# Conditioning on 32x32 parts of the array, GpSimd casting the shared first weights, and a new deal of banks and of VectorE's first work

## The reference, cut to what matters

```python
w = weights[conditions]                       # 32 batches, each a 32x32 matrix
xc = einsum('bct,bcd->bdt', x, w)             # x is (32, 32, 256): 1024 tokens of 256
logits = xc @ gate_w; top 2 of 8 experts; capacity 160 tokens of an expert and choice
h = gelu(buf @ w1[e] + b1[e]); y = h @ w2[e] + b2[e] + gelu(buf @ wd[e]) @ wu[e]
sh = gelu(xc @ sw1 + sb1) @ sw2 + sb2 + gelu(xc @ swd) @ swu
out = x + sum over the 2 choices of weight * y + 0.2 * sh
```

## Time and profile before

| | us |
|---|---|
| three runs | 180.92, 179.42, 179.10 (median 179.42) |
| the profiled execution | 179.35 |
| its span (first to last instruction) | 177.6 |
| TensorE busy | 172.2 |
| VectorE, ScalarE, GpSimd busy | 149.7, 145.7, 96.4 |

### The profile page before, as it was taken

How to read it: one execution, slowest core, us unless ns; L and a number is a source line. 1 busy time by engine, 2 the same in 40 slices (tenths; PEclk the granted TensorE clock), 3 DMA queues, 4 the chain that set the end, 5 groups by cost and what they waited for, 6 DMA issues and landing times.

```text
span 177.6 us, 4056 instructions
## 1 busy us (share of the span) xinstructions
PE 172.2 (97%) x1410; PEld 167.5 (94%) x1410; DVE 149.7 (84%) x332; ACT 145.7 (82%) x323; POOL 96.4 (54%) x110
## 2 busy tenths in 40 slices
PE   5899999999999999999999999999999999999994
PEld 5797789999999999999999999999999999999993
DVE  5578999999996989879889699898999999989822
ACT  3369889805878997998899799999899999998920
POOL 5900448310447663087977948868947555264700
PEclk9999999999999999999999999999999999999999
DMA  4595000749938493595788859579688778686232
GB/s 129 128 351 174 0 0 2 242 145 315 326 76 304 111 303 84 238 251 68 258 289 120 284 161 182 134 278 229 142 292 191 196 258 151 238 259 75 29 65 94
DMA packets 25885, 31.84 MB, mean 179 GB/s; under 512 B 4572, under 2 KB 22392, under 8 KB 25864
## 3 DMA queue, kind: packets, MB, share of 16 engines
q1 hardware_dynamic: 21720, 26.22, 46.0%
q0 software_dynamic: 3904, 5.25, 16.7%
q10 hardware_dynamic: 240, 0.10, 0.2%
HBM read 26.31 MB, written 5.24 MB: 178 GB/s over the span
## 4 chain that ended last, share of the span: by engine, by line
PE 91%; DVE 4%; DMA 3%; issue 1%; DVEq 0%
PE y_ps L1040 14%; PE y_ps L1039 14%; PE y_ps L1038 14%; PE hid_ps L1038 9%; PE hid_ps L1039 9%; PE hid_ps L1040 9%; PE turn_ps L1038 4%; PE turn_ps L1040 4%; PE turn_ps L1039 4%; PE turn_ps L1207 2%; DMA cond_g<-in_L_cond_weights,itok_col 2%; PE hid_ps L1066 1%; DMA itok_col<-in_itok_B 1%; PE turn_ps L1066 1%; PE row_ps L1223 1%
## 5 line engine op out<-in xcount | busy, mean ns | idle before, releaser
L733 DVE TENSOR_TENSOR hid_l<-gelu_f,hid_h 128x320 fp32r<-128x320 f32 (+2 forms) x88 | 43.6, 510 | 10.9 <-ACT hid_h L628 10.2
L477 POOL DMA_INDIRECT out_rows<-y_row,slot_tok x23 | 38.1, 1655 | 24.7 <-DVE y_row L919 10.1
L463 POOL DMA_INDIRECT slot_in<-slot_rows,slot_src x23 | 31.0, 1348 | 18.4 <-DVE slot_src L889 7.9
L1038 PE MATMUL y_ps<-w_h,hid_h 128*128 128x256 f32 (+2 forms) x128 | 36.2, 283 | 0.0
L1039 PE MATMUL y_ps<-w_l,hid_h 128*128 128x256 f32 (+2 forms) x128 | 36.1, 282 | 0.0
L1040 PE MATMUL y_ps<-w_h,hid_l 128*128 128x256 f32 (+2 forms) x128 | 36.1, 282 | 0.0
L1038 PE MATMUL hid_ps<-xs_h,w_h 128*128 128x248 f32 (+6 forms) x96 | 27.6, 287 | 0.0
L627 ACT ACTIVATE gelu_f<-hid_ps,bias_s 128x320 f32<-128x320 f32 x48 | 26.2, 546 | 1.3 <-PE hid_ps L1040 1.1
L1039 PE MATMUL hid_ps<-xs_l,w_h 128*128 128x248 f32 (+6 forms) x96 | 27.2, 283 | 0.0
L1040 PE MATMUL hid_ps<-xs_h,w_l 128*128 128x248 f32 (+6 forms) x96 | 27.2, 283 | 0.0
L710 DVE TENSOR_TENSOR w_l<-w_raw,w_h 128x512 fp32r<-128x512 f32 x40 | 27.1, 712 | 0.0
(11 more groups left out here) (240 smaller groups left out, 445.6 us busy)
## 6 DMA issues: line engine op xcount, KB each, us to landing
w_raw<-in_L_ffn_w SPq DMA_DIRECT2D x16, 1024.0 KB, 5.2
w_raw<-in_L_ffn_sw SPq DMA_DIRECT2D x3, 1024.0 KB, 5.3
x_in<-in_x SPq DMA_DIRECT2D x2, 512.0 KB, 3.8
w_raw<-in_L_ffn_sw SPq DMA_DIRECT2D x2, 512.0 KB, 6.0
slot_rows<-token_row SPq DMA_DIRECT2D x2, 512.0 KB, 4.1
wu_raw<-in_L_ffn_wu SPq DMA_DIRECT2D x24, 32.0 KB
out_rows<-base SPq DMA_DIRECT2D x1, 512.0 KB, 4.8
slot_in<-slot_rows,slot_src POOLq DMA_INDIRECT x23
```

The lines of the kernel that those rows point to most:

```text
L463: pool.indirect_dma_start(out=slot_in[par][0:n, s, :], out_offset=None, in_=x_rows, in_offset=bass.IndirectOffsetOnAxis(ap=slot_src[0:n, e ...
L477: pool.indirect_dma_start(out=out, out_offset=bass.IndirectOffsetOnAxis(ap=slot_tok[0:n, e, s:s + 1].bitcast(U32), axis=0), in_=y_row[0:n, ...
L733: dve.tensor_tensor(hid_l[:, j - 1, 0:n], gelu_f[:, j % 3, 0:n], hid_h[:, j - 1, 0:n].bitcast(F32), ALU.subtract).then_inc(hid_split, 1)
L1038: pe.matmul(out_ap, l_h, r_h, start=start, stop=False)
```

## The change

Seven things are done at once.

1. `cond_diag` goes. The blocks lie in `cond_b` (32 columns for each tile), and 32 float32 matmuls of a 32x32 stationary block by 32x256 of `x_in`, 16 for each half, write token *rows*: block `g` of a tile reads partitions 32g to 32g+31 and writes partitions 32t to 32t+31 of bank `g` of its half (`tokens_ps`).
2. ScalarE and VectorE each copy two of a half's four banks to `token_row`, 16 transposes (1077) turn these into the old `xct` layout, in `xct_ps`, and the casts and remainders are read from there with a reordered pattern. `make_rows`, `keep_xct` and the late `copy_rows` go.
3. The rows go to HBM in eight transfers right after they are copied, not in two after the hidden tiles.
4. GpSimd casts all four chunks of the shared first weights; ScalarE casts none, and makes the two copies of the scores.
5. `hid_banks` is dealt anew for the shared tiles, `COUNT_AT` becomes 5 and `MAP_AT` 4, the ring of gelu buffers has five entries (the two new ones in `cond_g`), and the first output tile waits for an earlier gelu.
6. VectorE does its four `w1_chunk` in a row, and the first split between the two choices; one more split stands ahead of `side_data`.
7. SyncE waits for the first half of `x_in`, not for `cond_g`, before it issues the second half. Gelus, input casts and remainders of the sixth and later ranks of experts are cut to the most tokens such a rank can have (`MOST`; 292 and 256 columns in place of 320 for the last two).

```diff
-COUNT_AT = 4
-MAP_AT = 2
+COUNT_AT = 5
+MAP_AT = 4
+RING = 5
+MOST = [min(SLOTS, K * T // (r + 1)) for r in range(E)]
@@
+        tokens_ps = [[hid_ps[2], y_ps[0], row_ps, turn_ps[1]], [hid_ps[0], turn_ps[0], hid_ps[1], y_ps[1]]]
+        xct_ps = [[hid_ps[2], row_ps], [hid_ps[0], hid_ps[1]]]
@@
             if u == 0:
-                six = [hid_ps[2], y_ps[1], y_ps[0], hid_ps[0], hid_ps[1], turn_ps[1]]
-                return six + six[:HT - len(six)]
+                return y_ps + [hid_ps[2], hid_ps[0], hid_ps[1], row_ps, hid_ps[2], hid_ps[0], hid_ps[1]]
             if u == 1:
-                return [row_ps] + [hid_ps[j % 3] for j in range(1, HT)]
+                return [turn_ps[1]] + [hid_ps[j % 3] for j in range(1, HT)]
@@
-            sp.wait_ge(cond_in, 16)
+            sp.wait_ge(x_loaded[0], 16)
             sp.dma_start(x_in[:, HTILES:NT, :], x_v[:, HTILES:NT, :]).then_inc(x_loaded[1], 16)
@@
+            for c in range(CHUNKS):
+                pool.wait_ge(w1_in if c < CHUNKS // 2 else w1b_in, 16)
+                pool.tensor_copy(w1_h[0][:, :, c * FC:(c + 1) * FC],
+                                 w1_raw[:, :, c * FC:(c + 1) * FC]).then_inc(w1_hi, 1)
@@
-                if u == 0 and j < 3:
-                    pass
-                else:
-                    act.wait_ge(hid_split, hid_count(u, j) - 3)
+                if hid_count(u, j) > RING:
+                    act.wait_ge(hid_split, hid_count(u, j) - RING)
@@
-                for k in range(KD):
-                    dst = hid_ps[k] if h == 0 else turn_ps[k]
-                    for t in range(HTILES):
-                        ins = pe.matmul(dst[:, t * P:(t + 1) * P], x_in[:, h * HTILES + t, k * P:(k + 1) * P],
-                                        cond_diag[:, h * HTILES + t, :], start=True, stop=True)
-                    ins.then_inc(xct_made, 1)
...
+                for t in range(HTILES):
+                    for g in range(SPT):
+                        block = slice(g * C, (g + 1) * C)
+                        ins = pe.matmul(tokens_ps[h][g][t * C:(t + 1) * C, 0:D],
+                                        cond_b[block, h * HTILES + t, :], x_in[block, h * HTILES + t, :],
+                                        start=True, stop=True)
+                ins.then_inc(tokens_made, 1)
+            for h in range(2):
+                for i, g in enumerate(ROWS_TURNED):
+                    pe.wait_ge(rows_by_act, h * len(ROWS_ON_ACT) + i // 2 + 1)
+                    pe.wait_ge(rows_by_dve, h * len(ROWS_ON_DVE) + i // 2 + 1)
                     for k in range(KD):
...
+                        ins = pe.transpose(xct_ps[h][k][:, g * P:(g + 1) * P],
+                                           token_row[:, h * SPT + g, k * P:(k + 1) * P], ident[:, :])
```

More of the change, by code:

```diff
@@ L58 @@
 ON_ACT, ON_POOL = (3, 2), (1, 0)
+ROWS_ON_ACT, ROWS_ON_DVE = (0, 1), (2, 3)
+ROWS_TURNED = (0, 2, 1, 3)
 OUT_OF_REACH = -1.0e30
@@ L374, in _ @@
             for h in range(2):
[L375 to L377 removed]
+                sp.wait_ge(rows_by_act, (h + 1) * len(ROWS_ON_ACT))
+                sp.wait_ge(rows_by_dve, (h + 1) * len(ROWS_ON_DVE))
+                for t in range(HTILES):
+                    sp.dma_start(x_rows_v[h * HTILES + t], token_row[t * C:(t + 1) * C, h * SPT:(h + 1) * SPT, :]).then_inc(
+                        x_rows_out[h], 16)
             load_first(1)
@@ L645, in _ @@
                         "p (k e) -> p k e", k=K), ACT.Copy).then_inc(used_copied, 1)
-            for b in range(NT // 2):
-                copy_rows(b)
             act.wait_ge(centred, 1)
@@ L738, in _ @@
             dve.wait_ge(cond_spread, 1)
+            for g in range(SPT):
+                dve.tensor_copy(*spread_part(g)).then_inc(blocks_dve, 1)
             for h in range(2):
-                for g in range(SPT):
-                    dve.tensor_copy(*spread_part(h, g)).then_inc(diag_dve, 1)
+                dve.wait_ge(tokens_made, h + 1)
+                for g in ROWS_ON_DVE:
+                    dve.tensor_copy(*row_part(h, g)).then_inc(rows_by_dve, 1)
             dve.wait_ge(gate_in, 16)
@@ L943, in _ @@
             wu_part(0, 0)
-            for j in range(6, HT):
-                split_tile(0, j, HALF)
-                if j < HT - 1:
-                    w2_chunk(j - 6, 0, 0)
+            w2_chunk(0, 0, 0)
+            split_tile(0, 6, HALF)
+            w2_chunk(1, 0, 0)
+            split_tile(0, 7, HALF)
             w2_chunk(2, 0, 0)
             w2_chunk(3, 0, 0)
+            split_tile(0, 8, HALF)
             place_tokens()
@@ L1044, in _ @@
             with pe.Fori(0, WARM_UP) as _:
-                for _ in range(10):
-                    pe.matmul(y_ps[0][:, 0:P], ones[:, :], ones[:, :], start=True, stop=True)
+                for i in range(10):
+                    pe.matmul(y_ps[0][:, i % 4 * P:(i % 4 + 1) * P], ones[:, :], ones[:, :], start=True, stop=True)
             pe.wait_ge(ident_made, 2)
@@ L1102, in count_before, with shared_low @@
                 ins.then_inc(pos_made, 1)
+            def shared_low(h, x_h, x_l, cols, n):
+                pe.wait_ge(gate_lo, 1)
+                dst = hid_bank(h, 0)[0:LOW_GATE, 0:n]
+                for k in range(KD):
+                    pe.wait_ge(xct_hi, h * KD + k + 1)
+                    pe.matmul(dst, low_gate_h[:, k, :], x_h[:, k, cols], start=(k == 0), stop=False)
+                    pe.matmul(dst, low_gate_l[:, k, :], x_h[:, k, cols], start=False, stop=False)
+                for k in range(KD):
+                    pe.wait_ge(xct_lo, h * KD + k + 1)
+                    ins = pe.matmul(dst, low_gate_h[:, k, :], x_l[:, k, cols], start=False, stop=(k == KD - 1))
+                ins.then_inc(hid_made, 1)
             def hidden(u, j, par, v, x_h, x_l, cols, n):
@@ L1255, in _ @@
                         map_slots()
-                if h == 0:
-                    for b in range(NT // 2):
-                        make_rows(b)
                 if h == 0:
```

199 lines of the change are left out of this document (86 added, 113 removed).

## The result

The changed kernel takes 186.1 us (median of 6 runs, 185.74 to 187.85) against 180.21 us for the kernel before beside it (6 runs, 179.1 to 181.22). The ratio is 1.034, with an interval of 1.027 to 1.040. A second comparison later, on another chip, gave 1.033 (1.027 to 1.039). The prediction was 178.5 us in a range of 177.3 to 183.9, so it was too low by 7.6 us, and the time lies outside the range.

A forecast was written before the change was run, and what follows sets the result against it. TensorE bounds the kernel, busy 172.2 of 177.6 us. First hidden tile +0.6, dropped transposes -1.66, dropped wait -0.16, new gather wait +0.3 give -0.9 against 179.35: 178.5 us, 8-in-10 range 177.3 to 183.9.

The forecast's parts named there:

- C: Time of the 32 small conditioning matmuls on TensorE, shown by no row; taken as 2.3 us.
- The other estimate, 1.4: Small matmuls: 14.5/10.6 = 1.4 us from the Trainium skill's speedup for 16 tiles, ending 0.9 earlier.
- Every part of the array works by itself: Small matmuls: time set by issuing alone, 64 records 0.033 us apart plus 0.2, 2.3 us; the case taken.
- four at a time: Rival on the small matmuls: only those with different input partitions overlap, 3.6 us, total 179.8; chance 0.10.
- in order: Rival: a small matmul's two records run one after the other and block what follows, 7.5 us, total 183.7; chance 0.20.
- no overlap: Rival: the small matmuls don't overlap at all, 14.5 us, total 190.7; chance 0.05.
- R: End of the small matmuls on TensorE, 8.5 + C = 10.8 us; token copies, casts and remainders were timed from it.
- Bounds of the stall 0 and 0.9; I take 0.3: TensorE's new wait for expert 0's gathered inputs, wanted at 51.5 with gathers before landing at 52.09; 0.3 us.
- The first rival: Small matmuls overlap, but VectorE or the gather is later; each slowed step adds 0.4 us, four give 180.0; chance 0.08.
- the sum: Changes to TensorE's stream against 179.35 us: +0.6 - 1.66 - 0.16 + 0.3 = -0.9, so 178.5 us.
- No clock to win: TensorE's granted clock already stands at 9 tenths or more in every slice, the 2.4 GHz level.
- more is won: Rival: short block copies, C at 2.1, no stall, choice of experts alone on its port; 1.1 lower, 177.4; chance 0.15.

The follow-up runs named there:

- e2: Changed kernel with SyncE's load of expert rank 2's first weights held until expert 0's gathers have landed; 183.67 us, ratio 1.017.
- e9: Changed kernel with a VectorE memset of 256 columns ahead of rank 1's four w1_chunk subtractions; 178.9 us, ratio 0.989.
- e16: Changed kernel with a VectorE memset of 448 elements ahead of rank 1's subtractions, the kernel of e14 timed in more rounds; 177.85 us, ratio 0.988.
- e7: Changed kernel with VectorE waiting for expert 0's three gather issues before rank 1's w1_chunk, and side_data behind the second split; 178.07 us, ratio 0.989.
- e14: Changed kernel with a VectorE memset of 448 elements ahead of rank 1's subtractions; one run, span 174.7 us.
- e11: Kernel of e7 with the load of rank 2's first weights held until the slots are in; 178.59 us, ratio 0.988.
- e15: Changed kernel with side_data and first bias sort before second-pass splits, MAP_AT 3, rank 2's first weights' load held until slots are in; 179.09 us, ratio 0.987.
- e1: Changed kernel with VectorE waiting for expert 0's three gather issues ahead of rank 1's four w1_chunk; 178.82 us, ratio 0.987.
- e8: Changed kernel with the two loops around the 32x32 matmuls swapped, so neighbours share input rows; one execution, 187.73 us.

## Why the prediction was wrong, by its own steps

- **C was right in kind and too large.** Taken as 2.3 us from the 32x32 record of the earlier trace rows; 1.47 measured up to the first transpose, and 1.91 in the slow start. The other estimate, 1.4, was nearer. "Every part of the array works by itself" holds; four at a time (3.6), in order (7.5) and no overlap (14.5) fell. The rival "in order" had a chance of 0.20 and carried most of the slower side; the strict program order that the Trainium skill gives in TensorE: Matmul & The Clock Gate, Part 3, is an order of starts and ends and did not show here as blocking: in a batch, records start 0.01 us apart and last 0.37 to 0.40, so that rival read more into it than the trace bears out.
- **The front.** First small matmul at 8.5 forecast, 8.21 measured; first hidden tile at 15.7, measured 14.79. The row numbers came at 44.81 + 0.18 = 44.99 in place of 46.2, and the slots were wanted at 50.75 in place of 51.5. The win of 1.95 us ahead of the slots was there, and more than was forecast (1.2). VectorE's work was sized well: from R (9.68 measured, by the first transpose; 10.8 forecast) to the row numbers it was 35.3 us, where the prediction had 35.4, so they came earlier because R did.
- **The step that failed is "Bounds of the stall 0 and 0.9; I take 0.3".** It compared the time at which TensorE wants the slots with the time at which the gathers land, and took for granted that three issues and the landing keep the 6.0 us (46.06 to 52.09) that they had. They took 56.63 - 44.99 = 11.6, up to GpSimd's next issue as before (TensorE went on at 56.42). The first rival ("VectorE or the gather is later") was in the right place, but its price came from a step of the choice that lost 0.4 beside GpSimd's casts, so from what GpSimd costs VectorE. What VectorE costs GpSimd was never priced.
- **The row that would have shown it was in the trace of before.** GpSimd's issues of later gathers there are long beside the same subtractions:

```profile
83.88 2.98 POOL L463 DMA_INDIRECT slot_in<-slot_rows,slot_src  x1 [0.30 <-issue]
```

  Three more like it follow, at 97.22, 111.42 and 125.17, of 2.99 us each. They cost nothing, since no one waits for them. From them a rival follows: the third issue for expert 0 under the run, 2 us late or more, 178.5 + 2 = 180.5 us and up, more if the weights' load gets ahead. The order of the two kernels shows the cause too: one more split stands ahead of `side_data`, so one less stands between the gathers and `w1_chunk`, and the gap of 50.29 - 50.00 = 0.29 us between issue and run in the kernel before was thin. No run puts back this one split alone.
- **Two costs that hang on the stall**: the load of rank 2's weights, released by the remainders and not by the gather (2.5 us, e2), and the clock behind the idle stretch, 0.50 and 0.68 over 4 us. Neither was in the sum. "No clock to win" was right, but there was clock to lose.
- With the hold gone the time would have come out inside the range, but not by the sum: e9, e16 and e7 measure 0.989, 0.988 and 0.989 of the kernel before, about 2 us less, where the sum had 0.9. On its base that is 0.989 x 179.42 = 177.4, at the low edge of the range and just the figure of the rival "more is won". That is in part luck: that rival had C at 2.1, and C came out at 1.5. The front is what the change wins; of the narrower gelus nothing shows, as e14, which has no wait, takes 174.7 - 50.35 = 124.4 us from the slots to the end, and the kernel before 124.9. Some 8 us, (1.034 - 0.989) x 180, were lost at one meeting of an issue and a run of subtractions.

The Trainium skill (SBUF — State Buffer, Who interferes with whom) says that a `tensor_tensor` with both inputs in SBUF contends with GpSimd's reads, but that in the probe behind the page it did not stall transfers issued by GpSimd as a copy did. The trace differs in the second part: here the issue of an indirect transfer took up to 4.08 us beside such subtractions. An indirect issue has row numbers to read (`slot_src`), which would fit the first part; no run here separates that. The lock that the Trainium skill describes in the same section, held to the end of one instruction, fits the mild cases above, which end some 0.8 us after one subtraction; it would not hold an issue for five. The measurement decides.

## What to carry to other kernels

Where GpSimd issues gathers that TensorE will wait for, look at what VectorE runs over each issue, not only at when the issue starts, and look in the old trace for long issues that cost nothing today. Put the row numbers early or the long subtractions behind a semaphore (0.2 to 0.9 us of VectorE's time here, against some 8 us): a fix by a small shift works, but hangs on tenths of a microsecond. And hold back a large load whose buffer comes free while a small urgent transfer is still to be issued: it gave back 2.5 us where the gather was late (e2), and nothing that could be measured where it was not (e11, e15).

## What was not expected of the hardware

- 64 records of 32x32 float32 matmuls, 256 columns wide, started in 1.1 us and were done in 1.5, each lasting 0.37 to 0.40.
- Two-input subtractions beside an indirect issue on GpSimd stretched it from 0.92 to 4.08 us, until five subtractions in a row were over. At other places of the same overlap it took 0.92 to 1.65. All long issues had a subtraction starting 0.18 to 0.26 us into them, and ended 0.8 to 0.9 us after the last subtraction of the run.
- A 1 MB load issued 1.2 us ahead of the end of the gather's issue made the landing 4.54 us instead of 2.04.
- Early in the kernel the same 20 matmuls took 1.28 us in some executions and 2.34 in others (e1, e8, e9, e11, e15), with the granted clock shown as 1.00 in both; the first small matmul then started at 9.57 to 9.69, and at 8.21 to 8.60 elsewhere. Comparisons of one execution against another in the first 12 us have to look at these rows first.
